# A recommendation tower on one core: weights loaded in chunk 1's look-ups, first loads in another order, turns moved later in a chunk with layers between them, VectorE sharing the last evictions

## The reference, cut to what matters

```python
B, D, F = 2048, 128, 26                      # samples, width, sparse fields
e = stack([tbl_f[ids[:, f]] for f in range(26)], axis=1)
combined = concatenate([dense[:, None, :], e], axis=1)          # 27 vectors a sample
interactions = einsum('bnd,bmd->bnm', combined, combined)
z = concatenate([dense, interactions[:, triu_i, triu_j]], axis=1)   # 128 + 351
h = concatenate([z, dense], axis=1)                                  # 607
h = maximum(h @ W_top1 + b_top1, 0)          # 512
h = maximum(h @ W_top2 + b_top2, 0)          # 256
y = h @ W_top3                               # 1
```

## Time and profile before

| | |
|---|---|
| time, median of 3 runs (lowest to highest) | 377.78 us (376.63 to 378.38) |
| span of the profiled execution, first to last instruction | 375.2 us |
| around the span (median less span; the execution's own time is not listed apart) | 2.6 us |
| PE busy | 329.8 us (88%), 6,048 matmuls |
| POOL busy | 258.0 us (69%) |
| DVE busy | 198.1 us (53%) |
| ACT busy | 191.4 us (51%) |
| mean granted TensorE clock | 0.968 of full speed |

### The profile page before, as it was taken

One profiled execution on the slowest core, in us unless ns is written; L12 is line 12 of the kernel. 1 busy time (PEld: TensorE's weight loads), 2 busy tenths in 40 slices (PEclk: granted clock), 3 DMA queues, 4 the chain that ended last, 5 costly groups with the idle time before them and its releaser, 6 DMA issues.

```text
span 375.2 us, 13452 instructions
## 1 busy us (share of the span) xinstructions
PE 329.8 (88%) x6048; PEld 297.8 (79%) x6048; DVE 198.1 (53%) x364; ACT 191.4 (51%) x234; POOL 258.0 (69%) x280
## 2 busy tenths in 40 slices
PE   0476856999989999999999999999899988999797
PEld 0475745998779978997799878997799867997586
DVE  3599741995049901993079704990099405940000
ACT  2587633456544655455444653465535563455323
POOL 6777777777777777777777777777777777774000
PEclk9998985999999999999999999999999999999969
DMA  6997492663236623662266324752266225423140
GB/s 158 258 260 183 119 317 55 140 207 90 51 91 148 199 52 76 141 211 63 61 141 198 92 59 96 191 145 59 70 149 196 73 54 127 112 56 71 35 67 2
DMA packets 55415, 45.72 MB, mean 122 GB/s; under 512 B 39444, under 2 KB 45179, under 8 KB 55359
## 3 DMA queue, kind: packets, MB, share of 16 engines
q1 hardware_dynamic: 45783, 26.91, 28.8%
q0 software_dynamic: 8704, 17.84, 18.0%
q10 hardware_dynamic: 871, 0.11, 0.2%
HBM read 37.91 MB, written 6.93 MB: 120 GB/s over the span
## 4 chain that ended last, share of the span: by engine, by line
PE 52%; POOL 25%; issue 12%; ACT 4%; DVE 3%; DMA 3%; ACTq 1%; SPq 0%; DVEq 0%
PE banks L441 27%; POOL rows L399 25%; PE banks L460 7%; PE mlp L479 6%; PE moved L424 5%; PE mlp L489 4%; PE mlp L520 2%; DVE masks L682 2%; DMA hot_ids<-in_ids_of_field_dram 1%; DMA rows<-in_tbl_dram,ids_sb 1%; ACT vectors L771 1%; DVE low L669 1%; ACT vectors L754 1%; PE banks L531 1%; PE mlp L500 1%
## 5 line engine op out<-in xcount | busy, mean ns | idle before, releaser
L399 POOL DMA_INDIRECT rows<-in_tbl_dram,ids_sb x272 | 257.1, 945 | 83.8 <-issue 81.1
L682 DVE TENSOR_TENSOR masks<-hot_ids,row_of 125x512 fp32r<-125x512 int32 (+1 forms) x336 | 181.5, 614 | 17.9 <-PE banks L441 13.4
L441 PE MATMUL banks<-masks,high 125*128 125x256 f32 x592 | 151.3, 295 | 18.9 <-DVE low L669 18.9
L441 PE MATMUL banks<-masks,low 125*128 125x256 f32 x592 | 146.9, 287 | 0.0
L441 PEld LDWEIGHTS banks<-masks,high 125*128 125x128 f32 x592 | 116.2, 196 | 20.9 <-issue 16.3
L441 PEld LDWEIGHTS banks<-masks,low 125*128 125x128 f32 x592 | 116.3, 196 | 0.1
L771 ACT ACTIVATE vectors<-moved 128x384 f32<-128x384 f32 (+1 forms) x80 | 87.8, 1097 | 3.9 <-PE moved L424 3.5
L754 ACT ACTIVATE vectors<-banks 128x512 f32<-128x512 f32 (+1 forms) x40 | 44.6, 1114 | 77.8 <-PE banks L441 77.8
L460 PEld LDWEIGHTS banks<-vectors 128*27 128x27 f32 x4096 | 45.6, 107 | 29.7 <-issue 23.1
L460 PE MATMUL banks<-vectors 128*27 128x27 f32 x4096 | 54.8, 196 | 14.5 <-issue 10.2
L691 DVE COPY vectors<-dense_sb 128x256 f32<-128x256 f32 x8 | 3.5, 435 | 103.1 <-PE banks L460 103.1
(11 more groups left out here) (33 smaller groups left out, 56.6 us busy)
## 6 DMA issues: line engine op xcount, KB each, us to landing
hot_ids<-in_ids_of_field_dram SPq DMA_DIRECT2D x32, 256.0 KB, 5.1
scratch<-products SPq DMA_DIRECT2D x28, 169.0 KB
rows<-in_tbl_dram,ids_sb POOLq DMA_INDIRECT x272
features<-scratch SPq DMA_DIRECT2D x7, 351.0 KB
w_sb<-in_tbl_dram SPq DMA_DIRECT2D x3, 448.0 KB
scratch<-products SPq DMA_DIRECT2D x28, 42.2 KB
dense_sb<-in_dense_dram SPq DMA_DIRECT2D x8, 128.0 KB, 4.8
hot_ids<-in_ids_of_field_dram SPq DMA_DIRECT2D x8, 128.0 KB
```

The costliest lines, as they stand in the source:

```text
L399: pool.indirect_dma_start(rows[:, (tile * TILE_ROWS + v) % RING, :], None, tables[f][:, :], bass.IndirectOffsetOnAxis(ap=ids_sb[:, tile, f ...
L441: last = nc.tensor.matmul(banks[:, j % BANKS, m * CHUNK:(m + 1) * CHUNK], part[:, part_of(j * PAIR + m, k), :], masks[:, mask % MASK_RING, ...
L682: nc.vector.tensor_tensor(masks[:, mask % MASK_RING, 0:size], hot_ids[0:PART_ROWS, n % ID_RING, 0:size], row_of[0:PART_ROWS, row:row + 1]. ...
```

## The change

What it does, in five parts:

1. **First loads.** SP's first list has another order: table 2 goes ahead of the second hot ids, the ids of the tiles from 2 on (`load_ids(1, ...)`) and `load_dense(0)` go behind all tables. ACT prepares table 4 ahead of the first evictions, and table 8 ahead of batch (0, 3).
2. **Weights.** SP now also waits for the first mask used in `look_up(1, 1)` before it loads them; chunk 1's hot ids and dense go ahead of them. DVE sums the two parts ahead of the masks of `look_up(1, 4)`.
3. **Order in a chunk.** `look_up(i + 1, 0)` stands ahead of `multiply(i, 2)`; the turns of tile a all stand in their own chunk; `second_layer` stands right behind `first_layer(i - 1, 3)` with a turn behind each; `multiply(i, 2)` and `multiply(i, 3)` stand side by side. ACT's list follows.
4. **Waits.** `place_dense` and `keep_pair(c, 0)` wait for step 2 of the chunk ahead instead of its last step.
5. **The end.** DVE evicts the last step and all of the first half's layers (`keep_step`, `keep_last` on DVE); ACT evicts the second half's, and issues two of the four quads of the second half's scratch writes.

The diff, cut to its core (the ACT list follows PE's in the same manner):

```diff
-                for q in range(QUADS if half == 0 else QUADS - 1):
+                for q in range(QUADS if half == 0 else QUADS // 2):
                     write_quad(sp, LAST, q, scratch_written, half)
...
             load_table(0)
             load_table(1)
-            load_ids(1, slice(TILES, ALL_TILES))
+            load_table(2)
             load_hot_ids(0, 1)
-            load_table(2)
             load_table(3)
...
             load_hot_ids(0, 4)
+            load_dense(0)
+            load_ids(1, slice(TILES, ALL_TILES))
+            for j in range(HOT_PAIRS):
+                load_hot_ids(1, j)
+            load_dense(1)
 
             sp.wait_ge(low_made, HOT)
+            sp.wait_ge(mask_used, MASKS + FIRST_MASK[1] + 1)
...
             def chunk(i):
+                a, b = TILES * i, TILES * i + 1
+                turn(a, 0)
+                look_up(i, 1)
                 last_layer(i - 2)
+                turn(a, 1)
+                look_up(i, 2)
+                turn(a, 2)
+                look_up(i, 3)
+                turn(a, 3)
+                look_up(i, 4)
+                turn(a, 4)
                 first_layer(i - 1, 0)
                 multiply(i, 0)
+                turn(b, 0)
                 first_layer(i - 1, 1)
                 multiply(i, 1)
+                turn(b, 1)
                 first_layer(i - 1, 2)
+                turn(b, 2)
                 first_layer(i - 1, 3)
+                second_layer(i - 1, 0)
+                turn(b, 3)
+                second_layer(i - 1, 1)
+                turn(b, 4)
+                if i == LAST:
+                    last_layer(LAST - 1)
+                else:
+                    look_up(i + 1, 0)
                 multiply(i, 2)
                 multiply(i, 3)
...
+            def keep_last(half):
+                firsts, seconds = MTILES1 * (LAST + half), MTILES2 * (LAST + half)
+                samples = samples_of(half)
+                dve.wait_ge(second_ready, seconds)
+                for m in range(MTILES1):
+                    dve.wait_ge(first_ready, firsts + m + 1)
+                    nc.vector.tensor_scalar(hidden1[:, m, samples], mlp[:, m % 2, 0:HALF], b1_sb[:, m:m + 1], 0.0,
+                                            ALU.add, ALU.max).then_inc(first_kept, 1)
...
+                    if i == 1 and j == HOT_PAIRS - 1:
+                        sum_weights()
                     make_masks(i, j)
             keep_dense(CHUNKS - 1)
+            keep_step(LAST, CHUNK_STEPS - 1)
+            keep_last(0)
...
-                    act.wait_ge(step_ready, c * CHUNK_STEPS)
+                    act.wait_ge(step_ready, (TILES * c - 1) * TILE_STEPS)
...
-            write_quad(act, LAST, QUADS - 1, last_written, 1)
-            for half in range(HALVES):
-                keep_last(half)
+            for q in range(QUADS // 2, QUADS):
+                write_quad(act, LAST, q, last_written, 1)
+            keep_last(1)
```

More of the change, by code:

```diff
@@ L562, in first_chunk @@
                 turn(1, 4)
+                look_up(1, 0)
                 multiply(0, 2)
@@ L585, in second_chunk @@
                 first_layer(0, 3)
+                second_layer(0, 0)
                 turn(3, 3)
[L587 removed]
+                second_layer(0, 1)
                 turn(3, 4)
[L589 removed]
+                look_up(2, 0)
                 multiply(1, 2)
[L591 removed]
                 multiply(1, 3)
[L593 removed]
             def chunk(i):
[L596 to L597 removed]
@@ L617, in chunk @@
+                turn(b, 4)
[3 more added lines that the diff above has]
+                    look_up(i + 1, 0)
                 multiply(i, 2)
-                turn(a_next, 0)
-                second_layer(i - 1, 0)
                 multiply(i, 3)
[L621 to L644, removed]
-                second_layer(LAST - 1, 0)
-                second_layer(LAST - 1, 1)
-                turn(b_now, 4)
-                last_layer(LAST - 1)
-                multiply(LAST, 2)
-                multiply(LAST, 3)
@@ L654, in _ @@
             second_chunk()
-            for i in range(2, LAST):
+            for i in range(2, CHUNKS):
                 chunk(i)
-            last_chunk()
             for half in range(HALVES):
@@ L795, in keep_first @@
                     act.wait_ge(second_ready, MTILES2 * c)
+                if m == 0 and c == 0:
+                    act.wait_ge(weights_loaded, 16 * WEIGHTS)
                 act.wait_ge(first_ready, MTILES1 * c + m + 1)
@@ L877, in first_chunk @@
                 keep_batch(1, 4)
+                keep_pair(1, 0)
                 keep_step(0, 2)
@@ L881, in second_chunk @@
             def second_chunk():
-                keep_pair(1, 0)
                 keep_batch(2, 0)
@@ L967, in _ @@
+                keep_second(i - 1, 0)
+                keep_batch(b, 3)
+                keep_second(i - 1, 1)
+                keep_batch(b, 4)
+                if i == LAST:
+                    keep_y(LAST - 1)
+                else:
+                    keep_pair(i + 1, 0)
+                keep_step(i, 2)
+                if i < LAST:
+                    keep_step(i, 3)
             first_chunk()
-            act.wait_ge(weights_loaded, 16 * WEIGHTS)
             second_chunk()
-            for i in range(2, LAST):
+            for i in range(2, CHUNKS):
```

126 lines of the change are left out of this document (45 added, 81 removed).

## The result

The changed kernel takes 390.14 us (median of 6 runs, 387.61 to 395.77) beside 378.08 us for the kernel before in the same session: ratio 1.0277, 95% interval 1.0234 to 1.032, which is 10.5 us. The profiled execution took 392.54 us, with a span of 390.4: 15.2 more than the 375.2 of before. What follows is read from it, and its parts therefore add up to some 5 us more than the ratio says.

What follows compares the result with a forecast made beforehand. PE and POOL were taken as nearly level, PE's last turn 6 us behind the gather floor. +7.0 + 3.1 - 1.5 + 1.7 - 2.5 - 1.4 = +6.4 on 375.2 gave 381.6, 384.2 with 2.6 us around it; range 372 to 391.

Steps and rivals of the forecast that it cites:

- the rival of the clock: The clock falls to 1.2 GHz at the pairs of multiplies: 394 us at six pairs, 389 at half; chance 0.17.
- The pair of multiplies: Adjacent multiplies outrun instruction packets: 1.35 us in each of chunks 2 to 6, 0.2 in chunk 1, +7.0 us.
- The rival that the fetch is hidden: PE's sequencer has asked for the packet before the pair starts, so pairs take 3.6 us or less: 374.0 us; chance 0.17.
- The second layer: Right behind the first layer, it waits for ACT's eviction: 0.56 us in chunks 2 to 6, 0.3 in chunk 1, +3.1.
- Start and weights: Chunk 0 gains 6.9 us, but first_layer(0, 0) waits 5 us as weights and scratch writes queue: net -1.5.
- Half clock after that wait: After the 5 us idle before first_layer(0, 0), the clock falls to 1.2 GHz: +1.7 us, bounds 0 to 3.4.
- Waits for rows: PE lags the gathers throughout, so its waits for gathered rows go: -2.5 us.
- The end: Shared scratch writes and evictions: load 1.0 us earlier, last step's eviction 0.4 quicker, -1.4 us.
- the end is not shared: DVE's evictions bring nothing at the end if the scratch round trip sets the time: 385.6 us, no chance given.
- gather floor: POOL's last gather issue at 341.55 plus 2.48 us landing: the last batch cannot come before 344.0.

Runs made afterwards that it cites:

- experiment 3: The changed kernel with a second layer between the last two multiplies in chunks 2 to 6, turns of tile b one place earlier: 383.13 us, ratio 1.0163.
- 10: The kernel of experiment 5 with multiplies 2 and 3 put side by side again in chunks 2 to 6: 384.28 us, ratio 1.0154.
- experiment 4: The changed kernel with multiply(i, 2) issued twice in chunks 2 to 6, so that three multiplies stand in a row: 411.64 us, ratio 1.0911.
- experiment 11: The kernel of experiment 5 with the second layer put right behind the first in chunks 2 to 6, the other between the multiplies: 380.96 us, ratio 1.0083.
- Experiments 6: The kernel of experiment 5 with the end as before the change: 375.86 us, ratio 0.9963.
- experiment 8: The changed kernel with the end as before the change: 391.39 us, ratio 1.0331.
- experiment 1: The changed kernel without SP's new wait for a mask ahead of the weights: 389.67 us, ratio 1.0342.
- experiment 2: The changed kernel with the weights held only until the first mask of look_up(1, 0): 390.29 us.
- experiment 5: The changed kernel without the new wait for the weights, multiplies 2 and 3 apart, the second layer not right behind the first: 376.2 us, ratio 0.9964.
- experiment 7: The kernel before with only the new order of the first loads: 376.95 us, ratio 0.9969.
- experiment 9: The kernel of experiment 5 with the weights held until the first mask of look_up(1, 0) and chunk 0's pair apart: 377.41 us, ratio 0.9982.

## Why the prediction was right in its direction and short in its size

The forecast was +6.4 us on a span of 375.2; the ratio says 10.5, the medians differ by 12.1, the profiled executions by 15.2. The direction held for the reasons given, the size did not: PE's last turn came at 363.63, not near 357. That 390.14 lies within 372 to 391 says little for the sum, since the top of that range was there for the rival of the clock.

- **The pair of multiplies (+7.0; right, measured +5.4).** The halts of chunks 2 to 6 are 1.0 to 1.3 us, 5.9 in all; chunk 1 halts 0.69 instead of 1.15, 0.5 less where 0.2 more was charged. Taking the pairs apart gave back 6.4 (experiment 3), putting them together cost 6.9 in halts (10), and a third multiply in a row halts longer still (4). The rival that the fetch is hidden, which the rule in "Runtime: NRT & Kernel Launch", section "Instruction fetch mechanics", of the Trainium skill would have given, fails at each. That the halts are waits for instructions, which the prediction inferred from the packets' size, is borne out by their times: each ends 1.2 to 1.6 us behind a packet of q8, and the packets never begin less than 3.3 us apart. What sets that distance stays open.
- **The second layer (+3.1; right).** Seven waits of 0.56, +3.2, and experiment 11 shows 2.8 of it alone.
- **Start and weights (-1.5; wrong sign, +1.6).** The queue was right: `look_up(1, 1)` began at 63.76 (forecast 63.8), and `first_layer(0, 0)` waited. The failed step is that the weights' data is through at 71.3 and the load issued at about 81. On SP's timeline of after, the writes and the wait for them took 13.9 us instead of 10.2, and on DVE's the weights are there at 75.89:

```profile
66.86 1.48 SPq L357 DMA_DIRECT2D w_sb<-in_W_top_dram  x2
68.38 1.21 SPq L357 DMA_DIRECT2D b_sb<-in_b_top_dram  x2
69.64 8.32 SPq L228 DMA_DIRECT2D scratch<-products  x8
83.51 0.30 SPq L285 DMA_DIRECT2D features<-scratch  x1
75.89 0.69 DVE L727 TENSOR_TENSOR w_sb<-w_sb,hidden 128x512 f32<-128x512 f32 x1 [1.64 <-DMA b_sb<-in_b_top_dram]
```

  The writes went out from 69.64 on, while the weights were still under way (share 0.98 in the stretch from 70 to 76). So the weights came 4.6 us later than forecast, the load went out 7.6 us after them instead of 10.2, and the two misses leave it at 83.51, not 81. It landed after 4.1 us instead of 3.3, and PE was ready at 80.8 instead of 79.0, so the wait is 6.8 us instead of 5. Of these 1.8 us, 1.3 have a cause that the prediction put at nothing: DVE's sum of the weights waited for them and held the masks of `look_up(1, 4)`, whose 20 matmuls began 0.47 us late and took 0.8 us longer than others do. It cost no time here, as the features came later still. Two smaller slips: 64.3 + 6.1 is 70.4 and not 71.3, and before, the first layer ran at 85.98, not 85.8.
- **Half clock after that wait (+1.7; measured +3.0)**, near its upper bound of 3.4: the low stretch of 10.2 us began while PE idled and held 6 us of its work. I had halved it without a row.
- **Waits for rows (-2.5; right)**, all gone.
- **Other halts (not in the sum).** Single multiplies and a turn halt 3.3 us in the middle (0.83, 0.30, 1.20 and the turn's 0.97) where before 1.17 stood (0.72 and a turn's 0.45). I had taken the pair to be the only place that changes, but other places of the new list also meet a packet that is late. That is +2.1, and two small waits make another 0.7.
- **The end (-1.4; measured +1.6).** The step "both are done after about 3.2: the load at 362.4 instead of 363.4" failed: issuing was not what set the load. In the changed kernel the load went out 6.21 us after the first write (371.64 to 377.85), before 5.97. Experiments 6 and 8 show no gain from sharing the end. The rival "the end is not shared" was the right one. The 1.6 us are the second half's layers, which met a low clock for 3.4 us (5.46 us at L521 instead of 3.84) in this execution; in that of experiment 8 they did not.

By these terms: 5.4 (pairs) + 2.1 (other halts) + 0.7 + 3.2 + 1.6 + 3.0 - 2.5 + 1.6 = 15.1 of the 15.2.

*The clock falls at each pair* (chance 0.17, 389 to 394) was half a rival. In the profiled execution of the changed kernel none of the pairs of chunks 1 to 6 brought the clock down. But the same pairs in other traces did: one in experiment 1, two in experiment 2, three in experiment 8, and each row of three in experiment 4. It differs from execution to execution of nearly the same list, so a forecast needs a share of pairs at which it happens, not yes or no.

**Where an expected gain could have gone.** Experiments 5, 6 and 7 end within 0.1% of each other, and experiment 9 within 0.2% of those. The best ratios are 0.4% below the kernel before, and the first loads alone give 0.3%, so no gain of the late turns can be told. In experiment 7 the lead goes into waits for gathers, as the prediction had read from rows 2 and 7. In experiments 5, 6 and 9 there is no wait for rows, and the last turn is still 4 to 6 us behind the gather floor of 344.0: there PE is held by its own halts for instructions (1.16, 1.66, 0.47, 0.27 and 0.70 us within y2 to y6 of experiment 5) and by the clock.

## What to carry to other kernels

When small matmuls are moved, count instructions between slower work, not only busy time: a row of 256 matmuls and 256 weight loads of 27 columns costs more than its halves apart, by a halt that no semaphore explains, and more still if the idle time brings the clock down. Where a profile gives "issue" as the cause of an idle time, look at the instruction queue: if the idle times end at a fixed distance behind its packets, they are waits for instructions. Before loading something "late", look at what stands behind it in the same queue, and let the two share bandwidth in the estimate instead of adding up only one of them. And splitting the issuing of transfers over two queues helps only where issuing, and not completion, is the last to end.

## What the runs showed of the hardware that was not expected

- All 118 halts by "issue" of 0.5 us or more after the first 44 us, in 13 traces, end 1.19 to 1.64 us after a packet of the instruction queue has ended. These packets, of 16.4 KB or about 252 instructions of PE each, never begin less than 3.3 us apart.
- In a row of three multiplies the second halt is longer than the first at all five places of experiment 4 (1.91 to 2.28 us against 1.28 to 1.74).
- One and the same halt, in `multiply(0, 1)` of chunk 0, is 4.15 to 5.61 us in the seven traces where the weights are loaded beside it (in experiment 1 the stretch from 48 to 56 has a DMA share of 0.89) and 0.60 to 1.60 us in the six where they are not.
- A halt of the same length does or does not bring the clock down: 1.42 and 1.46 us did (experiment 11), 1.81 us did not (experiment 9). The fall then lasts from 3.4 to 13.7 us in these traces, and 3.4 us of work at half clock costs 1.7.
- Four writes on each of two queues complete 6.1 to 6.2 us after the first is issued, six and two 5.9 to 6.25.
